# Graph network, building stage: two rows of bins in turn, places in pieces of two or three groups, two rows' sums in one PSUM bank

## The reference

```python
h = jnp.maximum(_layernorm(x), 0.0)
x = x + segment_sum(h[src], dst, 6250)                 # layer 0
h = jnp.maximum(_layernorm(x), 0.0)
out = h
for l in range(3):                                     # layers 1 to 3
    f1, f2 = relu(h_[src] @ nb_W[l] + nb_b[l]), relu(h_[dst] @ self_W[l] + self_b[l])
    log_alpha = relu(concat([f1, f2]) @ att1_W[l] + att1_b[l]) @ att2_W[l] + att2_b[l]
    mask = clip(sigmoid(log_alpha) * 1.5 - 0.45, 0, 1)
    vals = mask * d_inv_sqrt[src] * d_inv_sqrt[dst]    # from the mask's sums by src
    h_ = segment_sum(vals[:, None] * h_[dst], src, 6250)
    out = out + h_
return x + out
```

## Time and profile before

| | before |
|---|---|
| median of 3 runs | 4434.0 us (4422.53 to 4437.3) |
| the profiled execution's own time | 4420.38 us |
| its span, from first to last instruction | 4418.5 us |
| building stage, first load to last add_in | 541 to 1242 us, 343 units |
| mean granted TensorE clock | 0.947 of full speed |

### The profile page before, as it was taken

How to read it: one execution, slowest core, us unless ns; L and a number is a source line. 1 busy time by engine, 2 the same in 40 slices (tenths; PEclk the granted TensorE clock), 3 DMA queues, 4 the chain that set the end, 5 groups by cost and what they waited for, 6 DMA issues and landing times. The chain is left out here.

```text
span 4418.5 us, 256510 instructions
## 1 busy us (share of the span) xinstructions
PE 3818.8 (86%) x99277; PEld 3641.2 (82%) x99278; DVE 3743.0 (85%) x5930; ACT 1965.6 (44%) x4794; POOL 2440.8 (55%) x3237
## 2 busy tenths in 40 slices
PE   5888577877859999799988999979997999979997
PEld 4777477777739999788886999979886999978887
DVE  8999878888867888799995888789996788879998
ACT  5888466776731212255552121145553112125554
POOL 3655377777831222388982222279885122238887
PEclk8888799999979999899998999989998999989999
DMA  1000099999926777566653777656662677756665
GB/s 30 2 2 2 17 268 285 294 286 283 287 68 233 243 243 244 165 171 171 171 141 128 242 244 242 215 156 171 170 171 82 222 243 244 243 159 171 172 171 138
DMA packets 533726, 794.14 MB, mean 180 GB/s; under 512 B 67990, under 2 KB 467786, under 8 KB 533642
## 3 DMA queue, kind: packets, MB, share of 16 engines
q1 hardware_dynamic: 500714, 714.25, 51.3%
q0 software_dynamic: 32928, 78.72, 8.3%
HBM read 672.34 MB, written 120.42 MB: 179 GB/s over the span
## 5 line engine op out<-in xcount | busy, mean ns | idle before, releaser
L1370 POOL TENSOR_TENSOR message<-message 128x448 f32<-128x448 f32 x1029 | 1242.4, 1239 | 211.1 <-ACT message L1354 211.1
L1141 PE MATMUL pre_ps<-rows_a,hotT_a 128*128 128x64 bf16 x21609 | 1289.8, 194 | 45.2 <-DMA hotT_a<-hot_scratch 27.9
L1141 PE MATMUL pre_ps<-table,hotT_a 128*128 128x64 bf16 x21609 | 1290.6, 194 | 7.1 <-issue 6.9
L1141 PEld LDWEIGHTS pre_ps<-rows_a,hotT_a 128*128 128x128 fp8e4 x21609 | 1132.2, 98 | 52.7 <-issue 52.3
L1141 PEld LDWEIGHTS pre_ps<-table,hotT_a 128*128 128x128 fp8e4 x21609 | 1132.9, 98 | 8.0 <-issue 8.0
L1381 DVE TENSOR_TENSOR message<-message 128x448 f32<-128x448 f32 x1029 | 993.7, 966 | 69.3 <-POOL message L1370 69.3
L1221 DVE SCALAR_TENSOR_TENSOR weighed<-pre_ps,w 128x448 f32<-128x448 f32 x1029 | 643.1, 625 | 311.0 <-PE pre_ps L1141 219.2
L1354 ACT ACTIVATE message<-high_ps,mask 128x64 f32<-128x64 f32 x3087 | 699.8, 327 | 295.2 <-PE high_ps L1313 276.5
L1325 PE MATMUL sum_ps<-message,hot_b 128*128 128x192 bf16 x7203 | 783.9, 247 | 6.3 <-DVE message L1381 5.7
L1313 PE MATMUL low_ps<-table,hot_b 128*128 128x64 bf16 x12348 | 531.5, 193 | 160.6 <-DMA hot_b<-hot_scratch 65.3
L1189 POOL TENSOR_SCALAR fresh<-gate 128x49 f32<-128x49 f32 x147 | 35.3, 240 | 1114.8 <-ACT gate L1169 1114.8
(11 more groups left out here) (150 smaller groups left out, 4988.0 us busy)
## 6 DMA issues: line engine op xcount, KB each, us to landing
hotT_a<-hot_scratch SPq DMA_DIRECT2D x1029, 224.0 KB, 4.5
hot_b<-hot_scratch SPq DMA_DIRECT2D x1029, 224.0 KB, 2.8
hot_scratch<-hot SPq DMA_DIRECT2D x343, 336.0 KB, 10.3
hot_a<-hot_scratch SPq DMA_DIRECT2D x147, 784.0 KB, 5.1
places<-slots_scratch POOLq DMA_DIRECT2D x686, 112.0 KB, 6.8
out<-res SPq DMA_DIRECT2D x1, 1536.0 KB
slots_scratch<-bins SPq DMA_DIRECT2D x49, 16.0 KB, 1.4
raw<-in_src SPq DMA_DIRECT2D x1, 768.0 KB
```

The source lines that it names most:

```text
L1141: last = nc.tensor.matmul(pre_ps[g][:, j, :], hotT[:, b, g, end, j * P:(j + 1) * P].bitcast(FP8), table, start=end + part == 0, stop=end = ...
L1370: pool.tensor_tensor(message[:, g, :, 1, :], message[:, g, :, 0, :], top[:, g, :, 0, :, 1], ALU.subtract).then_inc(s["rest_ready"], 1)
```

## The change

The order of work becomes `each_unit`: row 0 alone, then 24 pairs of rows (row 1 with 2, 3 with 4, and so on). Within a pair the units alternate between its two rows: group 0 of the first row (`h` = 0), group 0 of the second (`h` = 1), group 1 of the first, and so on. The number of units, finds, turns, counts, add_ups and stores stays as it was, and so do the lags between them and the 7 slots of `hot`.

What differs is this:

- `places` holds two rows. The 7 groups come in three pieces (`chunks`): groups 0 and 1, groups 2 and 3, groups 4 to 6. A load is now 128 x 1792 or 128 x 2688 bytes instead of 128 x 896.
- `cnt_ps` and `sum_ps` have two buffers each.
- The add_ups of the two rows of one group run into the same PSUM bank, one after the other, without clearing it between, and DVE's add_in follows only the second (`h == 1`).
- `fetch_rows` (the copy of the row's table part by ACT) moves behind the copy of the counts of group 0, with a wait for `summed`.

```diff
-        places = sb("places", [P, NG, 2, G * P], U8)
+        places = sb("places", [P, 2, 2, NB * P], U8)
...
-        cnt_ps = ps("cnt_ps", [P, 8, P])
-        sum_ps = ps("l0_ps", [P, G, D])
+        cnt_ps = [ps(f"cnt_ps{i}", [P, 8, P]) for i in range(2)]
+        sum_ps = [ps(f"l0_ps{i}", [P, G, D]) for i in range(2)]
...
+                def load(c, h, r):
+                    a, z = chunks[c]
+                    for e in range(2):
+                        tile = k.slots_dram[bass.ds(r + e * k.HALF, 1), a * G:z * G, :]
+                        pool.dma_start(places[:, h, e, a * G * P:z * G * P],
+                                       tile.rearrange("r c e -> (r c e)").partition_broadcast(P))\
+                            .then_inc(places_in[c][h], 16)
...
+                with pool.Fori(1, (NB - 1) // 2) as i:
+                    for c, (a, z) in enumerate(chunks):
+                        for h in range(2):
+                            wait_count(pool, s, s["hotT"], NG + (i - 1) * (2 * NG) + 2 * (z - 1) + h + 1)
+                            load(c, h, i * 2 + 1 + h)
...
-                def add_up(q, r, g, b):
-                    pe.wait_ge(s["counts_ready"], q + 1)
-                    pe.wait_ge(s["rows_ready"], r + 1)
-                    pe.wait_ge(s["added"], q + 1)
+                def add_up(n):
+                    opens, closes = n.alone or n.h == 0, n.alone or n.h == 1
+                    pe.wait_ge(s["counts_ready"], n.u + 1)
+                    pe.wait_ge(s["rows_ready"], n.r + 1)
+                    if opens:
+                        back = 1 if n.g == 0 else 3 if n.g == 1 else 2
+                        at_least(pe, s["added"], n.m - back + 2)
+                    hold_waits(pe, s)
                     for j in range(G):
                         for part in range(PARTS):
-                            last = nc.tensor.matmul(sum_ps[:, j, :], counts[:, (b + g) % 2, j, :],
-                                                    rows[:, b, part * D:(part + 1) * D],
-                                                    start=part == 0, stop=part == PARTS - 1)
+                            last = nc.tensor.matmul(sum_ps[n.g % 2][:, j, :], counts[:, n.half, j, :],
+                                                    rows[:, n.h, part * D:(part + 1) * D],
+                                                    start=opens and j == 0 and part == 0, stop=closes and part == PARTS - 1,
+                                                    skip_group_check=True)
...
+                def add_in(n):
+                    if n.h == 1:
+                        dve.wait_ge(s["summed"], n.u + 1)
+                        part = k.one[:, n.g * G:(n.g + 1) * G, :]
+                        dve.tensor_tensor(part, part, sum_ps[n.g % 2][:, :, :], ALU.add).then_inc(s["added"], 1)
```

More of the change, by code:

```diff
@@ L37 @@
     pass
+Unit = namedtuple("Unit", "u r g h slot half uses m i alone")
 class Chain:
@@ L792, in _, with store @@
             @block.sync
             def _(sp):
[L794 to L801, removed]
+                def store(recent):
+                    n = recent[0]
+                    wait_count(sp, s, s["hotT"], n.u + 1)
+                    wait_count(sp, s, s["hot_ready"], n.u + 1)
+                    sp.dma_start(k.hot_dram[bass.ds(n.r, 1), :, n.g, :, :].rearrange("r p a b -> (r p) a b"),
+                                 hot[:, n.slot, 0:3, :]).then_inc(stored[n.slot], 16)
@@ L854, in _, with step @@
-                each_row(pe, NB, row)
-                count(Q - 1, NG - 1, 0)
-                add_up(Q - 2, NB - 1, NG - 2, 0)
-                add_up(Q - 1, NB - 1, NG - 1, 0)
+                def step(recent):
+                    for n, do in zip(recent, (turn, count, add_up)):
+                        if n is not None:
+                            do(n)
+                each_unit(pe, k, 3, step)
             @block.scalar
             def _(act):
-                def take_counts(q, g, b):
-                    act.wait_ge(s["counted"], q + 1)
-                    nc.scalar.activation(counts[:, (b + g) % 2, :, :], cnt_ps[:, 0:G, :], ACT.Copy)\
-                        .then_inc(s["counts_ready"], 1)
@@ L884, in _, with take_words @@
[L884 to L885 removed]
+                def take_words(n):
+                    act.wait_ge(s["turned"], n.u + 1)
+                    reused(act, n)
+                    at_least(act, s["counted"], n.u - NG + 1)
+                    nc.scalar.activation(hot[:, n.slot, 2:4, :].rearrange("p a e -> p (a e)").bitcast(I32),
+                                         word_ps[n.half][:, :, :, :].rearrange("p a j w -> p (a j w)"),
+                                         ACT.Copy).then_inc(s["hot_ready"], 1)
@@ new lines, in take_counts, with fetch_rows @@
+                def take_counts(n):
+                    act.wait_ge(s["counted"], n.u + 1)
+                    nc.scalar.activation(counts[:, n.half, :, :], cnt_ps[n.half][:, 0:G, :], ACT.Copy)\
+                        .then_inc(s["counts_ready"], 1)
+                    if n.g == 0:
+                        fetch_rows(n)
+                def fetch_rows(n):
+                    if not (n.alone or n.h == 0 and isinstance(n.i, int) and n.i == 0):
+                        act.wait_ge(s["summed"], n.u - 1)
+                    nc.scalar.activation(rows[:, n.h, :].rearrange("p (a d) -> p a d", d=D),
+                                         k.table_s[:, bass.ds(n.r, 1), :, :].rearrange("p r a d -> p (r a) d"),
+                                         ACT.Copy).then_inc(s["rows_ready"], 1)
@@ L909, in _, with find @@
-                each_row(dve, NB, row)
-                for back in (3, 2, 1):
-                    add_in(Q - back, NG - back)
-                dve.wait_ge(s["added"], Q + 1)
+                def find(n):
+                    dve.wait_ge(places_in[chunk_of[n.g]][n.h], n.i * 32 + 32 * (1 + n.h))
+                    reused(dve, n)
+                    dve.tensor_scalar(hot[:, n.slot, 0:2, :], places[:, n.h, :, n.g * G * P:(n.g + 1) * G * P], k.pcol1[:, 0:1],
+                                      float(HOT), ALU.is_equal, ALU.mult).then_inc(s["hotT"], 1)
```

129 lines of the change are left out of this document (56 added, 73 removed).

## The result

The change made the kernel about 1% faster: 4388.36 us median (4385.38 to 4393.12) against 4435.65 us, ratio 0.9902 with a 95% interval of 0.9888 to 0.9916. The ratio stands for 43 us, give or take 6; the two medians lie 47 us apart. Forecast were 65 us (4369 us).

The account below looks back on a forecast made before the run. DMA was taken to bound the building stage: 0.87 us loads plus 0.87 us store, 1.74 us at a share of 0.965, make 1.80 us a unit for 1.99; 0.19 x 343 = 65 us, 4434 - 65 = 4369 us, range 4325 to 4437.

Parts of the forecast that it names:

- DMA and not an engine bounds the stage: Building stage: DMA needs 1.92 us of a 1.99 us unit, DVE about 1.7 us, PE 1.59 us.
- the halved add_ins and second buffers are worth nothing by themselves: DVE's work falls from 1.77 to 1.47 us a unit, worth nothing while DMA needs 1.92; second PSUM buffers count zero.
- a jam of engines on the same bytes: Loads: 16 engines reading the same 896 bytes hinder each other; longer pieces spread them, so lost time shrinks, not vanishes.
- The fast slices of the earlier trace: First 6 us, loads alone: slices jump from 36 to 96 GB/s to 371 to 418 GB/s with the same 896-byte DMAs.
- rival 1: A load costs by its bytes, whatever the width: DMA stays at 1.92 us, time at 4434 us; chance 0.16.
- The 0.87 us for the loads: Engine time for a unit's loads, from 1.05 us: the middle of 1.05 (nothing gained) and 0.68 (a later stage's pace).
- at today's share of 0.965: DMA's share of the time, kept as before: 1.74 us of DMA time a unit gives a unit of 1.80 us.
- The find's wait for stores falls: Sign that the forecast is right: DVE's find waits less than 59 us in 600 for stores to land.
- `fetch_rows` costs zero: Moving ACT's row copy behind the copy of the counts costs nothing: 0.36 us in 14 us, ACT 71% busy.
- The other signs: If right, q0's (the loads' queue) share per MB falls by a sixth or more; PE's busy share rises to about 88%.
- Rival 3: Loads come in bursts, DMA's idle share rises from 4% to 10%: unit 2.13 us, 50 us slower, 4484 us; chance 0.10.
- Rival 2: The jam goes almost wholly; PE bounds at 1.59 us work plus 0.1 us gaps, 1.69 us; 4331 us; chance 0.22.

Follow-up runs that it names:

- narrow: The changed kernel with the places loaded in pieces of one group again (128x896); 4413.55 us against 4418.95 for the kernel before, ratio 0.9984.
- own_sums: The changed kernel with every unit's own add_up result and add_in again (343 add_ins), wider pieces kept; 4378.97 us against 4418.95 for the kernel before, ratio 0.9909.
- copies16_late14: The changed kernel with 16 copies of the bins, add_in one unit later and 14 slots of hot; 4289.68 us against 4403.10 for the kernel before, ratio 0.9747.
- pieces34: The changed kernel with two pieces of 3 and 4 groups instead of three; 4356.52 us against 4418.13 for the kernel before, ratio 0.9860.
- apart_narrow: The changed kernel with one-group pieces, each partition loading its own row of bins (output not the reference's); 4336.58 us against 4418.95 before, ratio 0.9811.

## Why the prediction was right, and its size not quite

- *DMA and not an engine bounds the stage; the halved add_ins and second buffers are worth nothing by themselves.* Right: narrow and own_sums.
- *The loads lose their time in a jam of engines on the same bytes, and longer pieces spread them.* Right, and shown as a part: with other addresses and the same widths the loads fell from 0.90 to 0.75 us and from 1.01 to 0.80. The fast slices of the earlier trace rows, from which it was read, fit what the packets show, a few long ones among many fast ones. But about half of the loss above the stores' pace stays with other addresses, and its cause is open. The rule of the Trainium skill ("DMA: Bandwidth & Descriptors", "Specifications": line rate from 512 bytes on) is half borne out: without the jam, 896-byte pieces cost only 0.05 us a unit more than wide ones; but that section says nothing of reads of the same bytes, so it could not stand for rival 1 here.
- *The size.* The 0.87 us for the loads was the middle of two far bounds; that 0.90 came out near it is in part luck. The forecast was 1.74 us of DMA time a unit in 0.965 of the time, 1.80 us. Measured were 1.79 in 0.94, 1.90 us. About half of the 0.10 us too few is the loads and stores (0.90 and 0.89 for 0.87 and 0.87), the other half the share that was taken as fixed, "at today's share of 0.965". (1.90 - 1.80) x 343 = 33 us of the 65 went that way. The 35 us of the stage are the 0.092 x 343 = 32 of the even part and 4 of its start and end; against them the stretch after the stage lost some 7.
- *The waits.* "The find's wait for stores falls" was wrong: it rose from 59 us in 600 to 70 in 580. A slot comes round sooner (7 x 1.90 = 13.3 us), and DVE, with half of its add_ins gone, comes to the store sooner. For the second speak two runs on one chip: the wait was 28.7 us in 550 with the add_ins back (own_sums) and 88.1 with them halved (narrow). A shorter engine in front of a full queue waits longer. That `fetch_rows` costs zero was nearly right: it brought PE 4.5 us of waits.
- *The other signs.* q0's share per MB fell by 15%, a little less than "a sixth or more". PE's busy share came to 82% and not 88%: a unit was longer, and PE was busy 1.54 us in it and not 1.59. That figure was no fixed need either; in copies16_late14 PE was busy 1.45 us a unit.
- *Rival 3, bursts.* The share fell, as its mechanism would have it, but pieces34 with larger bursts had 97%, as narrow had with small ones; what lowered it in the changed kernel stays open. 14 slots bring it to 98%.
- *Rival 2, PE as the bound with 1.69 us.* It was the right number for the case without the jam (1.71 to 1.72), but its reason was wrong and the number luck: not PE's own work and gaps, but a loop of DVE and PE through the add_in, which went when the add_in was put one unit later. The mean granted clock of TensorE was 0.99 to 1.00 of full speed from 600 to 1060 us in the runs without the jam, and 0.97 in the changed kernel; what share of their gain comes from it was not separated.

## What to carry to other kernels

When a queue's packets hold the engines but move few bytes, look at what they read before counting their number or width: here a broadcast that all 16 engines took from the same DRAM bytes went slower than the same load from distinct rows, and a few copies, stored where DMA is hardly used (4% before the stage), were worth more than wider loads and cost nothing that showed. Two bounds close together hide a third: after each one is removed, read the timeline of a stretch without DMA waits again, and take a pair of mutual waits in it as the next bound. Do not hold the share of a nearly full resource fixed in a sum. And a ratio to a kernel before does not make two chips alike, where they differ in the very stage that was changed: compare on one chip.

## What the runs showed of the hardware

- All partitions reading the same DRAM bytes: 1.01 to 1.06 us of engine time for 2 x 112 KB (0.90 with wide pieces), 0.76 with two copies, 0.73 with 16, 0.75 with 128 distinct rows. Two copies already take away four fifths of what 16 do, more than was expected.
- The time is lost in few packets: in the kernel before the load packets of 2688 bytes took 107 ns in the median and 210 in the mean, in apart_narrow 107 and 117.
- A store of 16 copies of 128x128 bytes for each of 49 blocks did not lengthen the sorting stage beyond the scatter: the first load after it is issued at 540.96 us, in the other kernels at 536.8 to 541.4.
- The kernel before took medians of 4400 to 4436 us on the chips used. By the traces of two of them, what lies outside the building stage took 3717 and 3719 us, so between these two the difference lies in the stage that is full of DMA.
